# Eight experts over every token, against tiles of the tokens that picked each expert

## What is computed

```python
def _L0_ffn_ref(x, router_w, gate_proj, up_proj, down_proj):
    NUM_EXPERTS = 8
    TOP_K = 2
    scores = jnp.einsum('btd,de->bte', x, router_w).astype(jnp.float32)
    probs = jax.nn.softmax(scores, axis=-1)
    routing_weights, routing_idx = jax.lax.top_k(probs, TOP_K)
    routing_weights = routing_weights / jnp.sum(routing_weights, axis=-1, keepdims=True)
    ...
    gate = jnp.einsum('bted,edf->btef', dispatched, gate_proj)
    up = jnp.einsum('bted,edf->btef', dispatched, up_proj)
    acts = jax.nn.silu(gate) * up
    expert_out = jnp.einsum('btef,efd->bted', acts, down_proj)
    return jnp.einsum('bted,bte->btd', expert_out, expert_w)
...
x = x + _L0_attn_ref(_layernorm(x, axis=-1), ...)
x = x + _L0_ffn_ref(_layernorm(x, axis=-1), ...)
x = x + _L1_attn_ref(x, ...)
x = x + _L1_ffn_ref(_layernorm(x, axis=-1), ...)
```

## Time and profile before

| | us |
|---|---|
| Median of 3 runs (2132.44 to 2137.86) | 2134.11 |
| The profiled execution, its own time | 2140.14 |
| Its span, first to last instruction | 2138.3 |
| PE busy in the span | 2001.0 |
| The experts, from their first to past their last product | 635 to 1160 |

### The profile page before, as it was taken

The page is one execution under the profiler, slowest core; times in us unless marked ns, Lnnn a source line. Parts: engine busy times, 40 slices in busy tenths (PEclk is TensorE's granted clock), DMA queues, the critical chain, the costliest instruction groups (busy, mean ns, idle before and its releaser), DMA issues. The chain is left out here.

```text
span 2138.3 us, 31115 instructions
## 1 busy us (share of the span) xinstructions
PE 2001.0 (94%) x11744; PEld 886.3 (41%) x11744; DVE 1462.6 (68%) x2435; ACT 1184.2 (55%) x2372; POOL 142.2 (7%) x216
## 2 busy tenths in 40 slices
PE   4599999999999999999998799999999999999876
PEld 2244444444436666666665212222222222222355
DVE  5577777777724554545555978888888888886276
ACT  2246666666662222322232337777777777777776
POOL 3100000000000000000000100000000000000165
PEclk9689999999999999999999769999999999999998
DMA  7633423433000000000000411001111110100000
GB/s 206 135 38 42 51 36 43 49 37 45 2 2 1 1 1 1 1 1 1 1 1 6 112 15 16 16 16 17 21 24 17 16 16 16 16 2 1 1 16 25
DMA packets 75268, 56.70 MB, mean 27 GB/s; under 512 B 43120, under 2 KB 57328, under 8 KB 75120
## 3 DMA queue, kind: packets, MB, share of 16 engines
q1 hardware_dynamic: 64416, 38.62, 12.9%
q0 software_dynamic: 3072, 10.23, 1.4%
q10 hardware_dynamic: 7632, 5.88, 1.0%
HBM read 38.65 MB, written 12.32 MB: 24 GB/s over the span
## 5 line engine op out<-in xcount | busy, mean ns | idle before, releaser
L1140 DVE TENSOR_REDUCE rowmax<-ps 128x1 f32<-128x1024 f32 (+7 forms) x1024 | 970.2, 987 | 245.3 <-PE ps L559 125.1
L909 ACT ACTIVATE probs<-ps 128x512 f32<-128x512 f32 (+3 forms) x1792 | 857.5, 557 | 338.6 <-PE ps L592 215.1
L559 PE MATMUL ps<-K,Q 72*128 72x512 bf16 (+3 forms) x1792 | 539.3, 376 | 27.8 <-DVE rowmax L1140 24.1
L592 PE MATMUL ps<-Q,K 75*128 75x512 bf16 (+3 forms) x1792 | 535.8, 361 | 12.9 <-ACT probs L909 8.7
L608 PE MATMUL ps<-probs,V 128*9 128x512 f32 (+3 forms) x3584 | 443.7, 552 | 0.0
L592 PEld LDWEIGHTS ps<-Q,K 75*128 75x128 bf16 x1792 | 165.3, 98 | 365.5 <-ACT probs L909 268.1
L945 ACT ACTIVATE Q<-ps 128x512 f32<-128x512 f32 (+1 forms) x192 | 114.4, 596 | 323.7 <-PE ps L718 312.1
L559 PEld LDWEIGHTS ps<-K,Q 72*128 72x128 bf16 x1792 | 152.4, 99 | 315.4 <-DVE rowmax L1140 166.4
L1251 DVE TENSOR_TENSOR Q<-ps,Q 128x512 f32<-128x512 f32 (+1 forms) x192 | 130.5, 687 | 141.5 <-PE ps L721 140.8
L721 PE MATMUL ps<-Q,wu 128*128 128x512 f32 (+1 forms) x384 | 196.7, 594 | 1.6 <-DVE Q L1251 1.6
L718 PE MATMUL ps<-Q,wg 128*128 128x512 f32 (+1 forms) x384 | 196.9, 594 | 0.7 <-DVE attn L1165 0.7
(11 more groups left out here) (157 smaller groups left out, 1122.6 us busy)
## 6 DMA issues: line engine op xcount, KB each, us to landing
Q<-q_parts SPq DMA_DIRECT2D x288, 64.0 KB
K<-k_parts SPq DMA_DIRECT2D x144, 64.0 KB
q_parts<-Q POOLq DMA_DIRECT2D x16, 384.0 KB, 3.4
k_parts<-Q POOLq DMA_DIRECT2D x8, 384.0 KB, 7.3
V<-v SPq DMA_DIRECT2D x16, 144.0 KB
K<-k_parts SPq DMA_DIRECT2D x144, 16.0 KB
x<-in_L_attn_h_dram SPq DMA_DIRECT2D x4, 512.0 KB, 10.1
out_dram<-y SPq DMA_DIRECT2D x8, 256.0 KB, 2.3
```

Source lines behind the costliest of these rows:

```text
L559: last = pe.matmul(buf[:, c:e], Q[0:CROSS, slot, j, i * P:(i + 1) * P], K[0:CROSS, slot, kj, c:e], start=True, stop=not diag)
L592: last = pe.matmul(ps[:, bank, c:HALF], K[0:KROWS, q, kj, t * P:(t + 1) * P], Q[0:KROWS, q, j, h * HALF + c:(h + 1) * HALF], start=True, s ...
L909: act.activation(probs[:, (4 * m + j) % PR, c:HALF], ps[:, B_BANKS[(4 * m + j) % 3], c:HALF], ACT.Exp, scale=SCALE).then_inc(sl["exp_done" ...
L1140: dve.tensor_reduce(rowmax[:, par, 8 * j + i:8 * j + i + 1], score_a(i % 2)[:, 0:hd.keys(i)], AX, ALU.max).then_inc(sl["max_done"], 1)
```

## The change

Only the experts of the first layer change, with the routing ahead of them. Every token is now sent as a row to the two experts that it picked, and an expert computes only its rows. There are two halves of 2048 tokens (`NGRP` = 2, `GU` = 4 groups each).

1. `route` takes the place of `prepare`. Its steps are set by the table `ROUTE`: those of half 0 stand behind the pieces 0 to 11 of the last quad of `attention(0)` and just behind it (steps 12 to 23), those of half 1 between the tiles of half 0, three tiles apart. VectorE also ranks the experts (`rank_experts`), counts the rows ahead of each (PE: `PF`), makes the place of each row (`place_rows`), and from the totals a table of tiles (`tile_table`): for each of `TILES` = 39 tiles of 128 rows the expert and the first row.
2. `scatter_rows` on POOL writes the normalised tokens with their weights to a buffer in DRAM, `dispatch`, by indirect DMA: one for each tile of 128 tokens and each of the two choices, 32 to a half.
3. `experts()` runs over 39 tiles to a half, 78 in all, whatever the counts are. SP reads the tile's row and expert into registers and loads the tile and its weights (`load_tile`) into one of `TS` = 4 places. PE transposes it (`turn_tile`), multiplies by gate and up of the expert that a register names (352 columns each), transposes the product three times (`turn_acts`) and multiplies by `wd` (`down_tile`, three products of 128 columns). ACT makes `hT_tile`, the Silu, and the weighted result (`weigh_tile`). POOL writes each result tile to the buffer `returned` by indirect DMA (`scatter_tile`).
4. When all 78 tiles are out, SP loads the results back, group after group (`load_back`), and VectorE adds both choices to `x` (`combine`), followed by `statistics_rms(u)`; `BACK` and `TAKE` are empty, so none of this stands among the tiles.
5. During `attention(0)` POOL fills `dispatch` with finite numbers, 18 transfers of 1.18 MB, one after each of the first 18 half quads.

The core of the diff; the functions of ACT and DVE in a tile are cut to the lines that the steps speak of:

```diff
+F0P = 384
+NGRP = 2
+GU = NG // NGRP
+TILES = (2 * GU * GW + E * (P - 1)) // P
+CAP = GU * GW
+ROW = D + 2 * E
+TS = 4
...
+            def load_tile(g, t):
+                n = TILES * g + t
+                k = n % TS
+                if t == 0:
+                    sp.wait_ge(pre["tables"], g + 1)
+                    for v in range(GU):
+                        sp.wait_ge(scattered[v], 16 * 2 * GT * (g + 1))
+                if n >= TS:
+                    sp.wait_ge(ex["turned"], n - TS + 1)
+                    sp.wait_ge(ex["y_ready"], n - TS + 1)
+                    sp.wait_ge(ex["target"], n - TS + 1)
+                row = sp.value_load(row_of[0:1, g, t:t + 1], min_val=0, max_val=(E + 1) * CAP - P)
+                expert = sp.value_load(expert_of[0:1, g, t:t + 1], min_val=0, max_val=E - 1)
+                sp.dma_start(x_tile[:, k, :], dispatch[g][bass.ds(row, P), 0:D]).then_inc(tile_in[k], 16)
+                sp.dma_start(meta[:, k, :], dispatch[g][bass.ds(row, P), bass.ds(expert * 2 + D, 2)])\
+                    .then_inc(tile_in[k], 16)
+            def load_back(u):
...
+                if u % GU == 0:
+                    last = TILES * (u // GU + 1)
+                    for k in range(TS):
+                        sp.wait_ge(tile_out[k], 16 * len(range(k, last, TS)))
+                if u >= 2:
+                    sp.wait_ge(y_taken, u - 1)
...
+            def scatter_rows(u):
+                v = u % GU
+                pool.wait_ge(pre["indexed"], u + 1)
...
+                for choice in range(2):
+                    for k in range(GT):
+                        at = bass.IndirectOffsetOnAxis(ap=index[:, v, choice, k:k + 1], axis=0)
+                        pool.indirect_dma_start(dispatch[u // GU][:, :], at, rows[:, v, k, :], None)\
+                            .then_inc(scattered[v], 16)
+            def scatter_tile(n):
+                k = n % TS
+                pool.wait_ge(ex["y_ready"], n + 1)
+                pool.wait_ge(ex["target"], n + 1)
...
+                pool.indirect_dma_start(returned[:, :], at, y_tile[:, k, :], None,
+                                        bounds_check=2 * B * S - 1, oob_is_err=False).then_inc(tile_out[k], 16)
...
-            def experts(u, more):
-                for e in range(E):
-                    gate_up(u, e)
-                    if e:
-                        down(u, e - 1)
-                    if more and e in (1, 2, 5, 6):
-                        prepare(u + 1, (1, 2, 5, 6).index(e))
-                down(u, E - 1)
+            def experts():
+                pe.wait_ge(ex["padded"], 1)
+                turn_tile(0)
+                for n in range(NGRP * TILES):
+                    expert = gate_tile(n)
+                    if n + 1 < NGRP * TILES:
+                        turn_tile(n + 1)
+                    up_tile(n, expert)
+                    if n >= 1:
+                        turn_acts(n - 1)
+                    if n >= 2:
+                        down_tile(n - 2)
+                    if n < TILES:
+                        route(1, n)
...
+            def weigh_tile(n):
+                k = n % TS
+                act.wait_ge(ex["down"], n + 1)
...
+                if n >= TS:
+                    act.wait_ge(tile_out[k], 16 * (n // TS))
+                act.activation(y_tile[:, k, :], ps[:, 5, P:2 * P], ACT.Copy, scale=meta[:, k, 1:2])\
+                    .then_inc(ex["y_ready"], 1)
+            def experts():
+                take_tile(0)
+                for n in range(NGRP * TILES):
+                    if n >= 3:
+                        weigh_tile(n - 3)
+                    gate_tile(n)
+                    if n + 1 < NGRP * TILES:
+                        take_tile(n + 1)
...
+            def combine(u):
+                par = u % 2
+                xs = x[:, u * GT:(u + 1) * GT, :]
+                dve.wait_ge(y_loaded[par], 16 * (u // 2 + 1))
+                own.done(dve.tensor_tensor(xs, xs, y_in[:, par, :, 0, :], ALU.add))
+                tell(dve.tensor_tensor(xs, xs, y_in[:, par, :, 1, :], ALU.add), y_taken, u + 1)
+                statistics_rms(u)
```

More of the change, by code:

```diff
@@ new lines, with numbers @@
+LAST = 24
+SINES = 24
+BACK, TAKE = (), ()
+def numbers(engine, kinds):
+    tables, n = [], 0
+    for g in range(NGRP):
+        table = {}
+        for step in sorted(ROUTE[engine][g]):
+            for ev in ROUTE[engine][g][step]:
+                if ev[0] in kinds:
+                    table[ev], n = n, n + 1
+        tables.append(table)
+    return tables
+TURNS = numbers("tensor", ("T1", "T2"))
+SMALL = numbers("tensor", ("WO", "LG", "PF", "TOT"))
+READS = numbers("vector", ("ADD", "SH", "IDX", "TAB"))
@@ L150 @@
+COPIES = numbers("scalar", ("CP1", "CP2"))
+for g in range(NGRP):
+    assert [n for n in SMALL[g].values()] == [n for n in READS[g].values()]
+    assert [({"WO": "ADD", "LG": "SH", "PF": "IDX", "TOT": "TAB"}[k], u) for k, u in SMALL[g]] == list(READS[g])
+    assert [({"T1": "CP1", "T2": "CP2"}[k], u) for k, u in TURNS[g]] == list(COPIES[g])
 LAYERS = [Heads(True, ORDERS[0]), Heads(False, ORDERS[1])]
@@ L375, in _ @@
                 batch(B - 1, True)
+                if l == 0:
+                    for g in range(NGRP):
+                        for t in range(TILES):
+                            load_tile(g, t)
+                            if g and t in BACK:
+                                load_back(BACK.index(t))
+                    for u in range(len(BACK), NG):
+                        load_back(u)
             for u in range(NG):
@@ new lines, in up_tile, with turn_acts @@
+            def up_tile(n, expert):
+                par = n % 2
+                if n >= 2:
+                    pe.wait_ge(ex["mul"], n - 1)
+                pe.matmul(ps[:, 2 + par, 0:F0], hT_tile[:, par, :],
+                          wu[:, bass.ds(expert, 1), :].rearrange("p a f -> p (a f)"),
+                          start=True, stop=True).then_inc(ex["up"], 1)
+            def turn_acts(n):
+                pe.wait_ge(ex["mul"], n + 1)
+                if n >= 1:
+                    pe.wait_ge(ex["act_ready"], n)
+                for c in range(len(FCH)):
+                    last = pe.transpose(ps[:, 4, c * P:(c + 1) * P], acts[:, n % 2, c * P:(c + 1) * P], ident[:, :])
+                last.then_inc(ex["act_turned"], 1)
@@ L808, in _ @@
             attention(0)
-            for u in range(NG - 1):
-                experts(u, True)
-            experts(NG - 1, False)
+            for step in range(LAYERS[0].G, LAST):
+                route(0, step)
+            experts()
             project(1)
@@ L1254, in accumulate @@
[L1254 to L1265 removed]
+                dve.tensor_tensor(rows[:, v, :, D + 1::2], rc[:, :, :], over_e(r2[:, :]), ALU.mult)
@@ new lines, in experts @@
+            def experts():
+                for n in range(NGRP * TILES):
+                    t = n - TILES
+                    multiply(n)
+                    if n >= 1:
+                        take_acts(n - 1)
+                        aim(n - 1)
+                    if t < 0:
+                        route(1, n)
+                    if t in TAKE:
+                        combine(TAKE.index(t))
+                    if t == SINES - 3:
+                        phases_terms()
+                    if t == SINES + 6:
+                        phases_coefficient()
+                take_acts(NGRP * TILES - 1)
+                aim(NGRP * TILES - 1)
+                for u in range(len(TAKE), NG):
+                    combine(u)
```

558 lines of the change are left out of this document (380 added, 178 removed).

## The result

| | before | after |
|---|---|---|
| Median of 4 runs each, us | 2135.99 | 2309.20 (2303.07 to 2310.39) |
| Ratio, 95% interval | | 1.0807 (1.0782 to 1.0833) |
| The profiled execution, its span | 2138.3 | 2307.4 |
| PE busy in the span | 2001.0 | 1845.3 |

The change makes the kernel 173 us slower; the forecast was 95. PE is busy for 156 us less and the kernel still takes longer.

A forecast was written before the change was run, and what follows sets the result against it. Prediction: PE bounds the old experts' stage; the new one is bound by a 6.65 us loop per tile through a load. Norm(0) 92 us later plus 3 for the fill made 95 more: 2229 us, range 2090 to 2375.

The forecast's parts named there:

- the first gate: Ahead of the tiles: first gate product at 679.4 us, 44 us later than before, behind POOL's 32 indirect transfers.
- second rival: Experts' tiles: the transfer is hidden and PE bounds at some 2.65 us a tile; 312 us less, 1917; chance 0.03.
- The period, 6.65: Loop of each tile through ACT, SP, load, PE and handing over: 6.65 us, 518.7 us for 78 tiles.
- 2.06 / 0.75: PE's part of the loop: 2.06 us at full clock, divided by a mean clock of 0.75, giving 2.75 us.
- third rival: Experts' tiles: the clock stays low, PE's part 4.12 us in place of 2.75; 107 us more, 2336; chance 0.14.
- first rival: Tile loop: cheap registers, load at its lower bound, full clock; period 4.96 us, 132 us less, 2097; chance 0.26.
- SP, 1.5: SP's part of the tile loop: two issues 0.6, two register loads 0.5, register instructions 0.4; sum 1.5 us.
- fourth rival: SP's part of the tile loop: register loads cost 1.0 us each; 117 us more, 2346; chance 0.11.
- The landing, 1.8: Tile loop: the 64 KB load takes 1.8 us to its landing, between bounds of 1.35 and 2.3.
- Routing of half 1 at nothing: Among half 0's tiles: routing lies in the engines' 4 us wait and costs nothing; fully exposed it would add 20 us.
- the step of 9.4 us: Behind the last tile: result, scatter, landing, load back and two additions delay the first statistics by 9.4 us.

The follow-up runs named there:

- eight places: Eight places for loaded tiles in place of four, results keeping four, against the changed kernel: 1979.2 us (ratio 0.9259).
- early registers: SP's two register loads for a tile moved ahead of the waits for the place, against the changed kernel: 2204.5 us (ratio 1.0335).
- warm half 1: Eight needless PE products of 128 columns behind each gate of half 1, added to the changed kernel: 2270.9 us (ratio 1.0630).
- early sums: BACK and TAKE filled, half 0 summed among half 1's tiles: changed kernel 2302.6 us; with eight load places and register loads ahead of the wait, 1966.2 us.
- spread scatters: Each group's eight half 1 scatters issued as 3, 3 and 2 behind three tiles, against the changed kernel: 2304.1 us (ratio 1.0771).
- more transfers: Sixteen more indirect transfers on POOL ahead of the first gate, 48 in place of 32, against the changed kernel: 2325.3 us (ratio 1.0892).
- without additions: The changed kernel without each group's two additions behind the last tile, statistics kept, one profiled run: 2305.6 us.
- five places: Five places for loaded tiles in place of four, results keeping four, against the changed kernel: 2023.5 us (ratio 0.9464).

## Why the forecast was right in sign and short in size

In the terms of the forecast, from its 95 us to the 169 between the spans (us): the first gate was 10.8 later than forecast, the tiles took 591.3 us in place of 521.7 (+69.6), the end was 5.9 shorter, and what follows norm(0) took 3.0 more where the forecast had nothing, and the fill took nothing where it had 3.

1. **The bound changes from PE to a loop through ACT, SP and a transfer: right.** The transpose is released by the load in the chain, and one more place made the kernel 286 us faster. That the second rival (PE bounds, 1917) was unlikely was right for this program; with eight places it holds, at 2.90 a tile in half 1 in place of 2.65.
2. **The period, 6.65: too short by one us, and PE's term is most of it.**

| us | forecast | changed | early registers | warm half 1 |
|---|---|---|---|---|
| PE, transpose to end of down | 2.75 | 3.60 | 3.02 | 2.21 |
| ACT | 0.35 | 0.38 | 0.40 | 0.38 |
| SP | 1.50 | 1.93 | 0.77 | 1.95 |
| landing | 1.80 | 1.70 | 1.67 | 1.99 |
| handing over | 0.25 | 0.05 | 0.05 | 0.05 |
| sum | 6.65 | 7.66 | 5.91 | 6.58 |

 Each column is one period (from 901.71, 1000.06, 1121.01). The mis-sized term is 2.06 / 0.75. The 2.06 at full clock was about right (2.21). The 0.75 was a mean of both levels, and the mean is the wrong number: the full level comes mostly in the pauses. Windows of the changed kernel, two of work and two of pause:

```profile
1016.00:1020.00 4.00, 3.60 (x13) 2.96 (x14) 1.15 (x3) 0.40 (x2) 0.00 (x0) 0.57 0.01 4
1020.00:1024.00 4.00, 0.58 (x2) 0.00 (x0) 0.00 (x0) 0.71 (x2) 0.97 (x1) 0.93 0.13 33
1024.00:1028.00 4.00, 3.80 (x13) 3.10 (x14) 1.15 (x3) 0.47 (x2) 0.00 (x0) 0.50 0.00 0
1028.00:1032.00 4.00, 0.94 (x2) 0.00 (x0) 0.00 (x0) 0.64 (x2) 0.97 (x1) 0.50 0.12 33
```

 PE's 3.6 to 3.8 us of work run at 0.57 and 0.50, and 0.93 is granted while PE has 0.58 us to do; in the other pause the clock stays at 0.50. The stage's mean of 0.66 to 0.71 is near the 0.75, and yet most of the work runs at the low level, 1.2 GHz: in 30 of 38 tiles of half 1 product up takes 1.17 us, in 1 some 0.6 as at the full level, and in 7 something between. With the needless products it takes some 0.6 in 37 of 38. That is the third rival's mechanism with a term of 3.6 in place of its 4.12; I gave it 0.14, and weighed it by how soon the clock came back in the earlier trace rows and not by whether there was work when it did. The earlier trace rows was also misread twice. The gap of 3 us is not shorter than what stood ahead of the low clock there: in the trace of the kernel before, PE paused 0.78 us ahead of its product at 2110.88 and 1.78 ahead of the one at 2113.82. That argument for the first rival was void. And the products that stayed at 0.50 in attention(1) are not short: they have 512 columns (L559). The rule of the Trainium skill ("TensorE: Matmul & The Clock Gate", Part 1), that the low level is the default and activity releases it, agrees: with the needless products the stretch is at 1.00.
3. **SP, 1.5: 0.43 short.** A register load is 0.26 us, as taken (0.25), but with its two instructions behind it and the gaps it is 0.55, and the first issue comes 0.15 after them. The fourth rival (1.0 each) is excluded. As cheap as a load looks, both together stood in the loop for 1.16 us, and moving them gave 105 us, with the share of the clock.
4. **The landing, 1.8: right** (1.70, 1.67, 1.99; the page lists 1.8 as the median of the 78).
5. **Routing of half 1 at nothing:** half 0 is only 0.1 a tile slower than half 1, as forecast. POOL's bursts pass in a loop of 7.7 us, as forecast, and no longer do in one of 3 to 4.
6. **Ahead of the tiles:** the first index at 641.97 (forecast 638), and scatters 1.26 apart in place of 1.1, 5 us in sum: the indirect one itself is 0.96, and 0.30 passes to the next. Another 1.05 pass from the index to the first of them. The last quad takes 58.5 us in place of 32.0 (601.72 to 660.24), 26 longer and not 8 or 9, and this cost nothing, beneath POOL's 41 us. By these ends (660.24 and 683.66) it would be the next bound if the scatters were cheaper.
7. **Behind the tiles:** the step that load_back waits for the last tile failed: those of groups 0 and 1 need half 0 alone, and their additions ran before PE's last down (statistics from 1280.74, last down over at 1281.46). Where a group of half 1 is first, the step of 9.4 us is there, at 8.8 (both kernels with early sums). Against this, each group took 6.4 in place of 5.9, by the additions beside POOL. Together the end, from the last down, is 46.4 us in place of 52.3.

**Open.** Half 0, the same program in the changed kernel and in the runs with needless products and with the early sums, took 12 us longer in those two profiles (distances of 9.8 to 12.3 between the transposes near tiles 12, 15 and 18), and no more than 3 us longer in the profiles with spread scatters, with more transfers and without additions. It is most of what the median of the needless products lacks against its expectation, and about half of it for the early sums. The long distances stand where POOL's bursts do, but two of the three profiles without them have the same bursts. What goes with them is the chip: from 600 us to the end of the tiles the four kernels of the first chip, and no others, have rows in which ACT and VectorE idle until a release that the profile calls "remote", without an engine or a transfer of this core. For ACT these sum to 28 us with early registers, 11 with needless products, 6 with the early sums and 46 with five places, all of them ahead of half 1's tiles. The kernel before is not slower on that chip. What those rows are isn't settled, and of the kernels tried only the kernel before ran on more than one of the three chips. So half 0's 6.76 and 4.73 of that chip may be too long, and the numbers of half 1 are the ones to trust. Nor is it settled why project(1) took 3.0 us more.

## What to carry to other kernels

When a change hangs each short step on a transfer, write down the loop from the giving back of a buffer to its next use, and count how many steps the buffers let it span; here four places let it span one tile (7.7 us) and five let it span two (6.6, so 3.3 a tile), and the fifth was worth 286 us, from 173 slower than before to 113 faster. What a queue does between its wait and its issue (two register loads) belongs in that loop, so do it ahead of the wait. Cost a pulsed TensorE at the clock granted in the windows in which it works, not at the stage's mean.

## What was unexpected of the hardware

- The full clock was granted mostly while TensorE paused (0.93 with 0.58 of 4 us busy) and was gone while it worked (0.57, 0.50). Eight needless products a tile held it at 1.00, and the half with more work was 51 us shorter.
- An indirect transfer of 128 rows holds POOL 0.96 to 0.99 us with 0.30 to the next, for rows of 576 bytes (the scatters) and of 512 (the results) alike.
- POOL's elementwise operations on 128 x 4 took 0.48 and 1.39 us beside VectorE's additions of 128 x 512, and 0.19 and 1.01 without them.
